# One preparation phase ahead of the edge count of a four-layer graph kernel

## The reference

```python
src, dst = src[argsort(dst)], dst[argsort(dst)]
x = ln(x + gat3(x, src, dst))             # three attention layers, one head, batch norm, relu
x = ln(x + gcn2(x, src, dst))             # two convolutions
x = ln(x + relgat(x, src, dst, etype))    # four heads, once for each of three edge types
x = ln(x + edge_attention(x, src, dst))   # and a feed-forward part
```

## Time and profile before

| | before |
|---|---|
| median of 3 runs | 2834.3 us (2833.37 to 2838.01) |
| profiled execution | 2861.6 us, its span 2859.7 us |
| head: start to first count matmul | 164.6 us |
| count loop | 164 to 597 us |
| the four networks | 597 to 2860 us |
| busy over the span: PE / DVE / ACT / POOL | 73% / 78% / 64% / 6% |

### The profile page before, as it was taken

How to read it: one execution, slowest core, us unless ns; L and a number is a source line. 1 busy time by engine, 2 the same in 40 slices (tenths; PEclk the granted TensorE clock), 3 DMA queues, 4 the chain that set the end, 5 groups by cost and what they waited for, 6 DMA issues and landing times. The chain is left out here.

```text
span 2859.7 us, 90081 instructions
## 1 busy us (share of the span) xinstructions
PE 2092.1 (73%) x33857; PEld 1846.2 (65%) x33857; DVE 2223.9 (78%) x4347; ACT 1831.8 (64%) x3004; POOL 158.2 (6%) x143
## 2 busy tenths in 40 slices
PE   0069978949959959939593998768995898766644
PEld 0045544638949949839482898768994898656622
DVE  2999978958878878761517999889997999849953
ACT  0059977957757666520205999599996999535421
POOL 0331133100000000000000000000000000000000
PEclk9979999979979979969796999889997999878867
DMA  2224534544314324227262333043312333034100
GB/s 80 87 86 189 229 158 163 225 159 125 123 63 142 106 90 147 73 65 226 77 210 77 107 102 91 17 127 95 108 56 81 104 101 97 8 105 128 57 8 23
DMA packets 186835, 308.74 MB, mean 108 GB/s; under 512 B 6718, under 2 KB 163265, under 8 KB 186446
## 3 DMA queue, kind: packets, MB, share of 16 engines
q1 hardware_dynamic: 185626, 303.77, 32.1%
q0 software_dynamic: 960, 1.26, 0.2%
HBM read 220.45 MB, written 88.67 MB: 108 GB/s over the span
## 5 line engine op out<-in xcount | busy, mean ns | idle before, releaser
L372 ACT ACTIVATE stage<-ps 125x375 f32 x625 | 314.0, 604 | 150.5 <-PE ps L317 146.1
L270 DVE TENSOR_SCALAR col<-iota_col,window_col 125x376 bf16<-125x376 f16 x1250 | 334.4, 336 | 33.4 <-PE ps L317 33.4
L317 PE MATMUL ps<-col,lo 125*125 125x375 bf16 x1250 | 288.1, 346 | 41.9 <-DVE col L270 41.7
L936 ACT ACTIVATE r2amsk<-r2ad,r2thr 125x640 f16 x360 | 259.9, 815 | 0.4 <-DVE r2asel L958 0.3
L936 ACT ACTIVATE r0amsk<-r0ad,r0thr 125x640 f16 x360 | 259.6, 814 | 0.1
L936 ACT ACTIVATE r1amsk<-r1ad,r1thr 125x640 f16 x360 | 259.6, 815 | 0.1
L1009 PE MATMUL ps<-r2mv,r2asel 125*128 125x66 f16 x5000 | 244.1, 196 | 6.6 <-issue 5.4
L317 PEld LDWEIGHTS ps<-col,lo 125*125 125x125 bf16 x1250 | 140.8, 141 | 163.0 <-DVE col L270 157.5
L1009 PE MATMUL ps<-r1mv,r1asel 125*128 125x66 f16 x5000 | 243.3, 196 | 2.7 <-issue 1.6
L1009 PE MATMUL ps<-r0mv,r0asel 125*128 125x66 f16 x5000 | 243.1, 196 | 1.3 <-DVE r0asel L958 0.5
L1009 PEld LDWEIGHTS ps<-r2mv,r2asel 125*128 125x128 f16 x5000 | 227.4, 100 | 10.4 <-issue 5.9
(11 more groups left out here) (532 smaller groups left out, 4480.8 us busy)
## 6 DMA issues: line engine op xcount, KB each, us to landing
counts<-stage SPq DMA_DIRECT2D x75, 800.0 KB, 4.8
ct<-counts_all SPq DMA_DIRECT2D x75, 800.0 KB, 4.6
counts_all<-total SPq DMA_DIRECT2D x25, 800.0 KB, 7.3
g0ct<-counts_all SPq DMA_DIRECT2D x25, 800.0 KB, 4.5
g1ct<-counts_all SPq DMA_DIRECT2D x25, 800.0 KB, 4.5
g2ct<-counts_all SPq DMA_DIRECT2D x25, 800.0 KB, 4.6
r0ct<-counts SPq DMA_DIRECT2D x25, 800.0 KB, 5.1
r1ct<-counts SPq DMA_DIRECT2D x25, 800.0 KB, 4.7
```

The costliest lines, as they stand in the source:

```text
L270: ins = v.tensor_scalar(col1[:, b % OHS * WIN + w], K.iota_col[:], K.window_col[:, bass.ds(i * (P // DG) + b, 1), w], None, ALU.is_equal)
L317: ins = pe.matmul(K.ps[0:P, s, 0:GW], lo1[:, b, 0:P, w], col1[:, s * WIN + w, 0:GW], start=(w == 0), stop=(w == WIN - 1))
L372: act.activation(dst.rearrange("p a r h d -> p (a r h) d"), K.ps[0:P, b % OHS, 0:GW].rearrange("p (x d) -> p x d", d=DG), ACT.Copy).then_i ...
L936: act.activation(msk[:, s % 5, n], ad[:, bass.ds(g % 2, 1), h] .rearrange("p a (b d) -> p (a b) d", d=PAD), ACT.Sigmoid, bias=T.thr[:, 1, ...
```

## The change

One phase, `prepare`, takes the place of the five.

- All loads go out at the start, the edges first; a tile of 125 partitions goes as two DMAs, of 112 and 13.
- GpSimd starts with an iota, then the memsets, selects and other iotas.
- `sub_range`, `lohi` and the comparisons of 4125 are gone. VectorE compares, for each of the 33 sub-runs of a partition, all 625 group numbers with that sub-run's highest group (`above`); TensorE adds over partitions and sub-runs with a matrix of ones; VectorE picks each partition's own five columns with the identity.
- The `windows` table is gone. The two windows of a group are 250 edges in one piece, and five indirect DMAs read them from `edge_keys` at a multiple of 25 edges.
- The flag comes from the gathered windows: edges that lie in their own group's column range are counted over all groups, and `wide` is set if they are fewer than all.
- The work of `score_weights` and `relation_weights` stands in VectorE's, TensorE's and ScalarE's programs between the counting and the gathered windows.
- `stage` and `total` are allocated ahead of the phase and cleared by ScalarE, as a Copy of `zeros`, before its Exp; GpSimd's clears and the waits for them in the count are gone.

```diff
@@ def prepare(nc, K, S), in place of prepare_edges and four phases
+    HEAD = 112
+    CUT = 63
+    SPLIT = (slice(0, HEAD), slice(HEAD, P))
+            def _(sp):
+                for h in SPLIT:
+                    sp.dma_start(ei[h, 1], K.dst_in.rearrange("(p c) -> p c", p=P)[h]).then_inc(dst_loaded, 16)
+                for k, edges in ((0, K.src_in), (2, K.typ_in)):
+                    for h in SPLIT:
+                        sp.dma_start(ei[h, k], edges.rearrange("(p c) -> p c", p=P)[h]).then_inc(src_loaded, 16)
...
+                sp.wait_ge(keys_ready, 2)
+                for h in SPLIT:
+                    sp.dma_start(K.edge_keys[:].rearrange("(p c) -> p c", p=P)[h],
+                                 K.keys[h].rearrange("p c k -> p (c k)")).then_inc(keys_out, 16)
+            def _(pool):
+                pool.iota(si[:], [[1, P], [P, DG]], channel_multiplier=0).then_inc(iotas, 1)
+                pool.memset(K.ident[:], 0.0).then_inc(cleared, 1)
+                pool.memset(K.ident16[:], 0.0).then_inc(cleared, 1)
+                pool.memset(K.zeros[:], 0.0).then_inc(made, 1)
...
-                pool.wait_ge(rows_ready, WIN)
-                pool.wait_ge(table, 16 * ROW)
+                pool.wait_ge(rows_ready, 1)
+                pool.wait_ge(keys_out, 32)
                 for j in range(DG):
-                    for w in range(WIN):
-                        pool.indirect_dma_start(win[:, j, w].rearrange("p e k -> p (e k)"), None, K.windows[0:NROWS],
-                                                bass.IndirectOffsetOnAxis(rows[:, j, w:w + 1], 0)).then_inc(gathered, 16)
+                    pool.indirect_dma_start(win[:, j].rearrange("p w e k -> p (w e k)"), None,
+                                            K.edge_keys[:].rearrange("(n e) -> n e", e=2 * SUB),
+                                            bass.IndirectOffsetOnAxis(rows[:, j:j + 1], 0)).then_inc(gathered, 16)
             def _(v):
+                link(v.memset(ones[:], 1.0))
+                v.wait_ge(iotas, 1)
+                link(v.tensor_copy(order[:], si[:]))
+                v.wait_ge(dst_loaded, 32)
+                link(v.tensor_copy(fd, ei[:, 1]))
...
+                link(v.tensor_reduce(top[:], q5[:].rearrange("p (c e) -> p c e", e=SUB), AX.X, ALU.max))
+                for c in range(NCH // SUB):
+                    v.tensor_scalar(above[:, c], order[:], top[:, c:c + 1], None, ALU.is_gt).then_inc(compared, 1)
...
+                for n, (c0, c1) in enumerate(((0, CUT), (CUT, P))):
+                    v.tensor_tensor(picked[:, c0:c1], K.ps[0:P, 5 + n, 0:(c1 - c0) * DG].rearrange("p (c j) -> p c j", j=DG),
+                                    K.ident[0:P, c0:c1].unsqueeze(2).to_broadcast([P, c1 - c0, DG]),
+                                    ALU.mult).then_inc(own, 1)
...
+                v.tensor_copy(rows[:], need[:]).then_inc(rows_ready, 1)
+                v.wait_ge(consts, 80)
...
+                v.wait_ge(relw_exp, 1)
...
+                v.wait_ge(gathered, 16 * DG)
...
+                link(v.tensor_scalar(seen[:], cols, float(GW), None, ALU.is_lt, ALU.add, accum_out=found[:, 0:1]))
+                link(v.tensor_scalar(seen[:], cols, 0.0, None, ALU.is_lt, ALU.add, accum_out=found[:, 1:2]))
...
+                v.wait_ge(shared, 1)
+                v.tensor_scalar(K.wide[0:1, :], found[0:1, 3:4], float(E), None, ALU.is_lt)
+            def _(act):
+                act.wait_ge(made, 1)
+                for tile in (K.stage[:].rearrange("p a r h d -> p (a r h d)"), K.total[:].rearrange("p a h d -> p (a h d)")):
+                    tile = tile.rearrange("p (n w) -> p n w", w=320)
+                    act.activation(tile, K.zeros[:, 0:320].unsqueeze(1).to_broadcast([ROWS, tile.shape[1], 320]), ACT.Copy)
+                act.wait_ge(relw_ready, 1)
+                act.activation(K.relw[:, 3:6], K.relw[:, 0:3], ACT.Exp).then_inc(relw_exp, 1)
             def _(pe):
+                pe.wait_ge(own, 1)
+                for c in range(NCH // SUB):
+                    pe.wait_ge(compared, c + 1)
+                    for n, (c0, c1) in enumerate(((0, CUT), (CUT, P))):
+                        ins = pe.matmul(K.ps[0:P, 5 + n, 0:(c1 - c0) * DG], ones[:], above[:, c, c0 * DG:c1 * DG],
+                                        start=(c == 0), stop=(c == NCH // SUB - 1))
@@ def count_edges(nc, K, S):
             def _(pool):
-                pool.memset(stage[:], 0.0).then_inc(cleared, 1)
-                pool.memset(total[:], 0.0).then_inc(cleared, 1)
@@
             def _(pe):
-                pe.wait_ge(cleared, 2)
@@
             def _(act):
-                act.wait_ge(cleared, 2)
```

More of the change, by code:

```diff
@@ L179, in _ @@
-                for w in range(WIN):
-                    link(v.tensor_scalar(need[:], wlo[:], float(NSUB - WIN * ROW), float(w * ROW), ALU.min, ALU.add))
-                    link(v.tensor_copy(rows[:, :, w], need[:]))
-                    v.sem_inc(rows_ready, 1)
-                for j in range(DG):
-                    link(v.tensor_scalar(cmp[:], lohi[:, 0], gf[:, j:j + 1], None, ALU.is_le, ALU.add,
-                                         accum_out=whi[:, j:j + 1]))
-                link(v.tensor_tensor(need[:], whi[:], wlo[:], ALU.subtract))
@@ new lines, in _ @@
+                v.wait_ge(own, link.n)
+                link(v.tensor_reduce(wlo[:], picked[:].rearrange("p c j -> p j c"), AX.X, ALU.add))
+                link(v.tensor_scalar(need[:], wlo[:], float(NSUB - WIN * ROW), None, ALU.min))
+                v.tensor_copy(rows[:], need[:]).then_inc(rows_ready, 1)
+                v.wait_ge(consts, 80)
+                link(v.memset(a[:], 0.0))
+                for l in range(3):
+                    v.tensor_copy(a[:, l, 0:2], K.cols[:, COL["a"] + 2 * l:COL["a"] + 2 * l + 2]).then_inc(filled, 1)
@@ new lines, in _ @@
+                for r in range(R):
+                    for h in range(4):
+                        part = slice(32 * h, 32 * h + 32)
+                        for side in range(2):
+                            c = COL["att"] + 2 * r + side
+                            v.tensor_copy(a[part, 3 + r, 4 * side + h:4 * side + h + 1],
+                                          K.cols[part, c:c + 1]).then_inc(filled, 1)
+                for n in range(2):
+                    v.wait_ge(wturned, 3 * n + 3)
+                    v.tensor_copy(wt[:, 3 * n:3 * n + 3], K.ps[:, n, 0:3 * D].rearrange("p (k f) -> p k f", f=D)
+                                  ).then_inc(wmoved, 1)
@@ L328, in five_groups @@
                             pe.wait_ge(taken, i * OHS + s + 1)
-                            pe.matmul(K.ps[:, s, :], K.zeros[:, 0:128], K.zeros[:], start=True, stop=True)
+                            pe.matmul(K.ps[:, s, :], K.zeros[0:P, 0:128], K.zeros[0:P], start=True, stop=True)
                             with pe.Fori(0, STEPS) as c:
```

227 lines of the change are left out of this document (78 added, 149 removed).

## The result

The changed kernel takes 2723.48 us (median; 2722.24 to 2725.16) against 2834.22 us: a ratio of 0.9609, with a 95% interval of 0.9596 to 0.9622, so 110.7 us less. The forecast was 2733 us with a range of 2717 to 2750.

The account below looks back on a forecast made before the run. The head of 164 us was to shrink ahead of an unchanged loop: 73.1 us from the phase ending earlier and 28.0 from the count's start, 101.1 off 2834.3, giving 2733 us, range 2717 to 2750.

Parts of the forecast that it names:

- GpSimd's opening: Start of the head: code load of 11.7 us ahead of the first iota, iota 0.9; `order` cast from 13.4 us.
- The keys: VectorE up to the keys: 9.9 us of operations, plus 1.5 for ones held beside GpSimd, to 24.8 us.
- The counting: Counting of sub-runs: 33 comparisons at 0.31 us, 10.2 in all, then matmuls and picks; `rows_ready` at 39.8 us.
- The gather: Five indirect DMAs, 1.55 us apart, the last issued at 46.0 us; landed at 50.5 us.
- ScalarE's clear: Clear of both staging tiles in the head: 30.1 us, from 14.4 to 44.5, covered by 3.6 us.
- The end: End of the phase, subtraction to copies: 59.4 us at TensorE's full clock, 61.3 at half; 60.0 taken.
- The start of the count: From the phase's end to the first count matmul: 3.0 us without GpSimd's clear instead of 31.0, 28.0 less.
- (a): Count loop: stalls fall otherwise, one more giving 2748 us (chance 0.12) or one fewer giving 2718 (0.05).
- (b): GpSimd's start: code load short or absent for the iota, VectorE 6 us or more earlier, 2727 us; chance 0.07.
- (c): Head: links taken at a middle value all fall high, giving 2742 us; chance 0.09.
- (d): Count loop: TensorE's clock stays at half and does not come back, 194 us lost, 2927 us; chance 0.02.
- (e): Edge check: too few edges found within the windows, so the wide path runs, some 240 ms; chance 0.01.

Follow-up runs that it names:

- clear_twice: The changed kernel with ScalarE clearing both tiles twice: 2748.9 us, run only once.
- own_phases: The changed kernel with constants, rows, score weights and relation weights in phases of their own ahead of it: 2750.2 us, ratio 0.9698.
- direct_only: The kernel before with only the direct read: no windows table, five indirect DMAs from edge_keys: 2834.9 us, ratio 1.0002.
- after_again: The changed kernel without edit, run again on another chip: 2724.2, 2724.8, 2725.1, 2733.5 and 2739.8 us.
- gpsimd_clear: The changed kernel with the clear of stage and total back on GpSimd at the start of the count: 2756.1 us, ratio 0.9707.
- gpsimd_clear_early: The changed kernel with the clear on GpSimd within the phase, after its iotas, instead of on ScalarE: 2761.1 us, ratio 0.9711.
- scalar_clear_only: The kernel before with only the clear moved, from GpSimd in the count to ScalarE during edge preparation: 2811.0 us, ratio 0.9892.

## Why the prediction was right, and where it was off

| link of the head | forecast | profile after |
|---|---|---|
| start to the iota for `order` ready | 13.4 | 10.0 |
| to both keys ready | 11.4 | 11.6 |
| to `rows_ready` | 15.0 | 15.4 |
| to the gather landed | 10.7 | 11.9 |
| to VectorE's first operation of the count | 11.5 | 9.6 |
| to the first count matmul | 1.5 | 1.3 |
| sum | 63.5 | 59.8 |

The mechanism of the prediction held: VectorE starts behind GpSimd's opening, the comparisons and the gather follow, the clear is covered, and the loop keeps its pace. The forecast of 2733 us is 9.5 too high; 3.8 of that lie in the head, nearly all in its first link, and the rest behind it. The other links agree in sum (50.1 and 49.8) partly by luck, as the gather was 1.2 us longer and the end of the phase 1.9 shorter.

- **GpSimd's opening** was the term that was mis-sized most. That a load of code moves ahead of the iota, and that VectorE starts behind it, was right; that it costs the 11.7 us of the earlier trace rows was not. It took 7.5 (records at 0.85, iota at 8.39), and the iota 1.6 instead of 0.9. The runs give 7.4 to 8.4 us ahead of an iota beside split loads, 9.3 and 9.7 beside unsplit ones, and 11.2 to 11.9 ahead of the affine select in four kernels. The Trainium skill (GPSIMD Engine Reference, section 2.1 Instruction dispatch) has some 6 us for the first call, which is nearer than my row and still below each of these; only the all-reduce's 6.0 agrees. What makes the affine select's longer than the iota's beside the same load of x stays open. And that the gap is a load of code is the reading, not a row: the profile shows an idle GpSimd behind two configuration records, and in the profiles before and after no packet of an instruction queue moves in the first 14 us.
- **The keys.** The sum of 9.9 and the 1.5 for operations held beside GpSimd's iotas came out within 0.2. The held ones are seen one by one: the tensor_scalar at 12.37 takes 0.98 instead of 0.59 us.
- **The counting.** 33 comparisons in 9.77 us (10.2 forecast), the reduce with its stride 1.27 instead of 0.8, and VectorE waits 0.80 for the last matmuls.
- **The gather** takes 5.1 us from the last issue to the use, with double bytes, where I had 4.5, and the five are 1.6 us apart.
- **ScalarE's clear**: 24.20 + 5.52 us, 0.84 ns per element, against 30.1 forecast. Its cover is 7.9 us (`clear_twice`), forecast 3.6; the difference is the opening again, from whose end the clear starts, and the Exp's table, which was loaded at the start.
- **The end** was a choice between a full and a half clock of TensorE, and the choice does not exist here. TensorE turned the windows in 4.51 us while its granted clock stood at 0.50 to 0.57 of full, and before in 4.56 us at full clock; `own_phases` and `clear_twice` took 4.54 and 4.56 at 0.50. That half the clock would double these transposes was wrong, and the middle value of 60.0 us held time for it. The second part is that VectorE's copies start 0.33 us apart instead of the 0.42 of their own length, as they overlap. The first row is the kernel before, the second the changed kernel (PEclk is the third number from the end):

```profile
128.00:133.00 5.00, 4.56 (x20) 4.28 (x20) 3.27 (x11) 0.00 (x0) 0.38 (x1) 1.00 0.00 0
...
50.00:55.00 5.00, 4.51 (x20) 4.28 (x20) 4.89 (x11) 0.00 (x0) 0.41 (x1) 0.53 0.00 0
```

- **The start of the count**: 28.2 us for the clear, 28.0 forecast, shown by undoing it and by doing it alone.

The head thus gives 104.9 us. Undoing one part at a time gives 28.6 for the clear and 26.7 for the merge; the remaining 49.6, found by subtraction, go to the new counting, the direct read and the new check together. Of these three the direct read alone gives nothing; the other two were not run apart.

The medians moved 110.7 us, 5.8 more than the head. The profile before had two stalls of 14.65 us in its loop, and I had taken the median to have none, which fits: 164.6 us of head with the later parts of the changed kernel's profile (401.7 and 2261.8) are 2828 us of span and 2830 with what lies around it, and the lowest runs before, over all chips, are 2827.5 to 2833.4. The medians before, 2832 to 2840, stand some microseconds over that. So the likely place of the 5.8 us is a share of such stalls in the timed runs before, and not the change. Two things speak for it. The profile of `direct_only`, whose loop and layers are those of the kernel before and whose head is 0.6 us shorter, fell on a run without a long add: 164.0 us of head, 403.7 of loop and 2262.6 to the end, a run of 2832.1 us, 106.9 above the profiled run of the changed kernel, while its other runs went up to 2862.7. And on another chip, `after_again` lies 107.6 us below the median of the kernel before, and their lowest runs are 104.8 apart, which is the head alone. But only one slow run of the kernel before was profiled, that with the two stalls; what the timed ones held is argued, not shown. The layers scatter too: from the last adds to the end it is 2265.2 us in the profile before, 2261.4 to 2262.6 in eleven others, with the old head as with the new, and 2258.2 in `own_phases`.

Of the rivals, (a), the stalls, did not happen in the median nor in a profile of the changed kernel; its two later runs 9 and 16 us above the lowest have the size, but no such run was profiled, and without the adds the runs still spread over 9.7 us. (b) was half true: the opening was 3.4 us shorter where (b) has 6 or more, and its gap did not go away. (c) did not happen, as the links behind the opening were 0.3 us under the forecast and not above it. (d), the clock: the first eight count matmuls took 2.77 us, as long as in the earlier trace rows, and 7.5 us after the first of them ten took 1.75 us, as in the earlier trace rows; it came back as before. (e) did not happen.

## What to carry to other kernels

Before pricing an idle engine's time as free, look at whose operations its work would stretch: a long GpSimd memset stretched the VectorE operation beside it by its whole length, and four small adds of together 2.1 us cost VectorE 0.7 us in each block, while ScalarE's 29.7 us of clearing cost nothing, being covered. Where two limits end together, removing one shows nothing until the other is gone; read what would be late next before leaving a part out as useless. A fixed cost at a program's start is worth its own row for each way of meeting it: the same kind of gap was 6, 7.5, 9.5 and 12 us in these kernels, and it hid transfers that the change had taken pains to speed up.

## What the runs showed of the hardware

**VectorE and GpSimd hold each other up, both ways.** A GpSimd memset of 24.1 us kept one tensor_scalar or one conversion waiting to its end (`gpsimd_clear`, `gpsimd_clear_early`). A two-input VectorE operation issued beside it was not held (0.82 us, the pair tile). The other way round, three small adds of GpSimd took 21.5 us in the middle of VectorE's one-hots, in two of 25 blocks. One block of `scalar_clear_only` had 21.55 us and one of `gpsimd_clear_early` 14.39. This is the one from `scalar_clear_only`, where the usual 1.7 us became 21.55, and the adds behind it:

```profile
363.77 21.55 POOL L256 TENSOR_TENSOR stage<-stage,ident 125x125 f16 x3 [13.60 <-ACT total L362]
385.74 1.17 POOL L256 TENSOR_TENSOR stage<-stage,ident 125x125 f16 x3
```

In the usual meeting both engines pay a little: the three adds take 1.7 us, against 1.17 with VectorE idle, and the ten one-hots beside them 3.0 us, against 2.35. In the stretched meeting VectorE pays nothing, and GpSimd's adds end 1.0 us after VectorE's last one-hot (all four that were seen). In the kernel before, the adds at 437.94 us (1.70) and at 469.35 us (21.54) had these beside them:

```profile
438.50 3.01 DVE L270 TENSOR_SCALAR col<-iota_col,window_col 125x376 bf16<-125x376 f16 x10
...
469.91 2.35 DVE L270 TENSOR_SCALAR col<-iota_col,window_col 125x376 bf16<-125x376 f16 x10
```

What decides between the two is open: the stretched adds began 15.7 us after the ones before them, like all others. The next ones came 22.0 us later, and in the kernel before the loop then stood still for 14.65 us.

**Turning 125 x 125 f32 windows does not follow TensorE's clock.** Twenty of them took 4.51 to 4.56 us at a granted clock of 0.50 to 0.57 and 4.56 at full clock. Count matmuls of 375 columns do follow it: eight took 2.77 us at 0.50, which is 0.35 each, and ten took 1.75 us at full clock, 0.175 each.
